# Routing the rows of a mixture of experts in five parts instead of two

## The chip, the cores and the metric

The kernel runs on one core of a Trainium2 chip. The metric is the device time of one execution in microseconds (us), the median of several runs. TensorE does the matrix products and transposes, VectorE (DVE in the profile) the elementwise work, ScalarE (ACT) activations and copies out of PSUM, GpSimd (POOL) issues the DMAs whose addresses come from a table in SBUF, SyncE (SP) issues the plain DMAs.

## The reference

The input is `x` of shape (2, 64, 64, 256), so two batches of 4096 tokens. A first layer (deformable attention with sampled keys and values) and an attention with one-dimensional convolutions come first; they take some nine tenths of the time and are not touched here. The last piece is a mixture of eight experts:

```python
logits = x @ gate_w + gate_b                      # x: 8192 tokens, 256 channels, after a layer norm
probs = softmax(logits)
idx = argmax(probs); prb = probs[idx]
one_hot = one_hot(idx, 8)
pos = (cumsum(one_hot, axis=0) * one_hot).sum(-1) - 1   # place of the token in its expert's list
kept = pos < C                                    # C = 1280 places for each expert
buf = zeros(8, C, 256).at[idx, pos].set(x)        # dropped where not kept
y = relu(buf @ w1 + b1) @ w2 + b2                 # expert by expert
out = t + y[idx, pos] * (prb * kept)
```

The place of a token depends on all tokens before it, through the running sum over the tokens. That sum can be made in parts, if each part begins with the counts that the parts before it have reached.

## The kernel before

`stage_mix_route` is the stage before the experts, `stage_experts` the last one. Each stage ends with a barrier over all engines (`Stage.__exit__`), and the expert stage begins with loads from `s["buf"]`, the table into which the tokens' rows are scattered. So all scatters have to be complete before the expert stage can start.

The mixing stage goes over 16 chunks of 512 tokens (`STEPS` = 16), eight for each batch; a chunk is four tiles of 128 tokens (`GT` = 4). Each loop step `n` runs on all engines:

- TensorE: `convolve(n)` (24 matmul records, the output projection), then `gates(n - 1)` (transposes of the normalized tiles and the gate logits of the chunk before), then `turn_out(n)` (transposes back to tokens by channels).
- VectorE: `share_out(n + 2)` (a product for a later chunk), `got_gates(n - 1)`, `residual(n)`, `normalize(n)`, which writes the rows `h` of the chunk.
- ScalarE: copies of `oT` and `hT` out of PSUM and the square root in `std`.
- SyncE stores the chunk and loads a later one.

Routing comes on top. `choose` (VectorE) finds each token's expert from the gates and leaves it as zeros and ones in `hot`. `count` (TensorE) multiplies `hot` by a triangular matrix and by a matrix of ones, which gives the running counts inside a tile and the totals of each tile in `ps_n`. `exponentials` (ScalarE) makes the exponentials of the softmax. `send` (VectorE) makes the token's probability, sums the tiles' totals in a scan that doubles its step, adds what is in `seen` from before, and writes the row number of each token to `to_row`. GpSimd waits for that (`rows_made`) and issues one indirect DMA for each tile of 128 tokens, which writes 128 rows of 264 numbers to `s["buf"]`.

Before the change this is done once for each batch: part 0 has the 32 tiles of batch 0, and its `choose` stands at step 8 and its `send`, `count` and `exponentials` at step 9. Part 1 has the 32 tiles of batch 1, and all of it stands behind the loop, since the last chunk's gates are needed. The order on each engine is the order in which the code is written; each engine waits only for semaphores.

Of the kernel before, what the change touches and what calls it, by code (L numbers as in the profile page):

```python
# [29 lines left out]
CHUNKS = N // CHUNK  # L30
# [10 lines left out]
E, F, CAP = 8, 4 * C, 5 * B * N // (4 * 8)  # L41
# [579 lines left out]
class Sampling:  # L621
# [235 lines left out]
    PARTS = 6  # L857
# [1253 lines left out]
def stage_mix_route(nc, d, s, keep, out):  # L2111


    with Stage(nc) as stack:
        r = Room(nc, stack, "x")
        ALL, GT, XS = B * TILES, CHUNK // P, 3
        STEPS, QS = B * CHUNKS, B * QBS
        inverse = Inverse(r, s, 1)
        ctx = [r.sb(f"ctx{b}", [P, CH, N + 2]) for b in range(B)]
        share = [r.sb(f"share{i}", [P, CH, QB]) for i in range(2)]  # L2120
# [3 lines left out]
        h = r.sb("h", [P, ALL, ROW])  # L2124
# [95 lines left out]

        @block.tensor
        def _(pe):
# [38 lines left out]
                            mm = pe.matmul(ps_g[:, i * E:(i + 1) * E], hT[i % 2][:, m, :], gw[:, m, :], start=(m == 0), stop=(m == CH - 1))  # L2261
                        mm.then_inc(g_mm, 1)

            def count(b):
                if b == 0:
                    pe.wait_ge(route_in, 80)
                else:
                    pe.wait_ge(count_got, b)
                pe.wait_ge(hot_made, b + 1)
                flat = hot[:, :, :].rearrange("p t e -> p (t e)")  # L2270
                pe.matmul(ps_n[:, 0, :], upper[:, :], flat, start=True, stop=True)
                pe.matmul(ps_n[:, 1, :], ones[:, :], flat, start=True, stop=True).then_inc(counted, 1)

            pe.wait_ge(edges, 2 * B)
            pe.wait_ge(consts, 80)
            for n in range(STEPS + 1):
                if n < STEPS:
                    convolve(n)
                if n:
                    gates(n - 1)  # L2280
                if n < STEPS:
                    turn_out(n)
                if n == CHUNKS + 1:
                    count(0)
            count(1)

        @block.scalar
        def _(act):
            def exponentials(b):
                act.wait_ge(less, b + 1)  # L2290
                act.activation(exps[:, :, :], exps[:, :, :], ACT.Exp).then_inc(exped, 1)
# [24 lines left out]
        def _(dve):  # L2316
# [43 lines left out]
            def tokens(v):  # L2360
                return v[:, :].unsqueeze(2).to_broadcast([P, TILES, E])

            def experts(v):
                return v[:, :].unsqueeze(1).to_broadcast([P, TILES, E])

            def tt(o, a, z, op):
                t.link(dve.tensor_tensor(o, a, z, op))

            def choose(b):
                gate = keep.gate[:, b * TILES:(b + 1) * TILES, :]  # L2370
                dve.wait_ge(g_got, CHUNKS * (b + 1))
                dve.wait_ge(route_in, 80)
                if b:
                    dve.wait_ge(rows_made, b)
                t.link(dve.tensor_reduce(top[:, :], gate, AX_X, ALU.max))

                tt(hot[:, :, :], gate, tokens(top), ALU.is_equal)
                tt(hot[:, :, :], hot[:, :, :], experts(prio), ALU.mult)
                t.link(dve.tensor_reduce(best[:, :], hot[:, :, :], AX_X, ALU.max))
                tt(rank[:, :, :], hot[:, :, :], tokens(best), ALU.is_equal)  # L2380
                dve.tensor_copy(hot[:, :, :], rank[:, :, :]).then_inc(hot_made, 1)
                dve.tensor_tensor(exps[:, :, :], gate, tokens(top), ALU.subtract).then_inc(less, 1)

            def send(b):
                own = slice(b * TILES, (b + 1) * TILES)
                dve.wait_ge(exped, b + 1)
                t.link(dve.tensor_reduce(total[:, :], exps[:, :, :], AX_X, ALU.add))
                t.link(dve.reciprocal(prob[:, :], total[:, :]))
                t.link(dve.tensor_copy(h[:, own, C], prob[:, :]))
                t.link(dve.tensor_copy(h[:, own, C + 1], number[:, own]))  # L2390
                dve.wait_ge(counted, b + 1)
                flat = "p t e -> p (t e)"
                t.link(dve.tensor_copy(each[:, :, :].rearrange(flat), ps_n[:, 1, :]))
                t.link(dve.tensor_copy(before[:, :, :], each[:, :, :]))

                step, src, dst = 1, before, work
                while step < TILES:
                    t.inc(dve.tensor_copy(dst[:, 0:step, :], src[:, 0:step, :]))
                    tt(dst[:, step:, :], src[:, step:, :], src[:, 0:TILES - step, :], ALU.add)
                    step, src, dst = 2 * step, dst, src  # L2400
                if b:
# [3 lines left out]
                tt(src[:, :, :], src[:, :, :], each[:, :, :], ALU.subtract)  # L2405
                dve.tensor_tensor(src[:, :, :].rearrange(flat), src[:, :, :].rearrange(flat), ps_n[:, 0, :], ALU.add).then_inc(count_got, 1)
                dve.wait_ge(count_got, b + 1)
                dve.wait_ge(hot_made, b + 1)
                tt(src[:, :, :], src[:, :, :], hot[:, :, :], ALU.mult)
                t.link(dve.tensor_reduce(place[:, :], src[:, :, :], AX_X, ALU.add))  # L2410
                tt(hot[:, :, :], hot[:, :, :], experts(first), ALU.mult)
                t.link(dve.tensor_reduce(expert[:, :], hot[:, :, :], AX_X, ALU.add))
                t.link(dve.tensor_scalar(kept[:, :], place[:, :], float(CAP), None, ALU.is_lt))

                t.link(dve.tensor_scalar(total[:, :], kept[:, :], -float(2 * E * CAP), float(2 * E * CAP), ALU.mult, ALU.add))
                t.link(dve.tensor_scalar(place[:, :], place[:, :], float(CAP - 1), None, ALU.min))
                tt(row[:, :], expert[:, :], place[:, :], ALU.add)
                dve.tensor_tensor(to_row[:, own], row[:, :], total[:, :], ALU.add).then_inc(rows_made, 1)

            t.link(dve.memset(h[:, :, C:], 0.0))  # L2420
            share_out(0)
# [15 lines left out]
            choose(1)  # L2437
            send(1)


def stage_attention(nc, d, s, keep, b, c, row_max, sa, begin, flow):
# [370 lines left out]
```

## Time and profile before

| | us |
|---|---|
| median of 3 runs | 9658.51 (9646.36, 9658.51, 9661.88) |
| the profiled execution, its own time | 9657.97 |
| its span (first to last instruction) | 9656.2 |
| TensorE busy | 7727.8 (80%) |
| VectorE busy | 5175.6 (54%) |
| GpSimd busy | 5070.2 (53%) |
| ScalarE busy | 3767.1 (39%) |

The span is what the timelines count from; 1.8 us of the execution's time lie outside it. The mixing stage's first TensorE instruction starts at 8684.43 us, the expert stage's first at 9027.93 us. The busy shares are means over stages with different limits, so the stretch around the change has to be read by itself.

### The profile page before, as it was taken

How to read it: one execution, taken by the hardware profiler on the slowest of the kernel's cores; microseconds unless marked ns; L12 is line 12 of the kernel's file. 1: busy time of each engine (PE TensorE's matmuls, PEld its weight loads, DVE VectorE, ACT ScalarE, POOL GpSimd, SP SyncE). 2: the span in 40 equal slices, each digit the busy share in tenths (PEclk: the TensorE clock that was granted, in tenths of full speed). 3: DMA queues.
4: the chain of work that ended last, by engine and by line, in shares of the span. 5: the costliest groups of instructions: out<-in, count | busy, mean ns of one | idle time of the engine just before them, and what ended most of it. 6: DMA issues, size and time to landing. Idle time of an engine off the chain costs nothing. (4 is left out here: it accounts for less than half of the span.)

```text
span 9656.2 us, 96652 instructions
## 1 busy us (share of the span) xinstructions
PE 7727.8 (80%) x31522; PEld 4168.2 (43%) x31522; DVE 5175.6 (54%) x10029; ACT 3767.1 (39%) x5495; POOL 5070.2 (53%) x4864
## 2 busy tenths in 40 slices
PE   7637776645894799869999977997999799989699
PEld 3623333433442344434444433443444344435466
DVE  6543335545564566656666555665653466634233
ACT  2101102201462266525666533662666255541232
POOL 1057777667777777777777777777730000001322
PEclk9868888867897799988999988997999799999799
DMA  3844335666543544454444355445430311115221
GB/s 129 289 150 137 120 119 178 213 217 211 161 138 112 175 138 144 130 179 126 138 139 146 119 176 180 142 129 178 137 101 28 94 46 46 40 45 157 81 73 54
DMA packets 658546, 1283.59 MB, mean 133 GB/s; under 512 B 189043, under 2 KB 398218, under 8 KB 643408
## 3 DMA queue, kind: packets, MB, share of 16 engines
q0 software_dynamic: 234240, 639.57, 21.2%
q1 hardware_dynamic: 405392, 562.58, 19.5%
q10 hardware_dynamic: 18432, 75.51, 2.0%
q8 instruction: 243, 3.98, 0.2%
q14 instruction: 239, 1.96, 0.1%
HBM read 1003.44 MB, written 278.91 MB: 133 GB/s over the span
## 5 line engine op out<-in xcount | busy, mean ns | idle before, releaser
L727 POOL DMA_INDIRECT sa_slot<-s_table,sa_rec x4608 | 4812.6, 1044 | 2279.2 <-issue 1382.9
L1704 DVE CUSTOM_DVE_ANT_0 a_above<-a_late,a_above 128x512 f32<-128x512 f32 x1600 | 1101.6, 689 | 1436.5 <-PE a_late L1556 1321.5
L1636 ACT ACTIVATE a_p<-a_s 128x1024 f32<-128x1024 f32 x1600 | 1628.6, 1020 | 124.4 <-PE a_s L1594 122.6
L1611 PE MATMUL a_ctx<-a_p,a_v 128*64 128x512 f32 x6400 | 1577.3, 614 | 85.0 <-issue 84.5
L1645 ACT ACTIVATE a_above<-a_diff 128x512 f32<-128x512 f32 x1600 | 956.6, 598 | 1648.2 <-PE a_diff L1544 1379.7
L769 DVE TENSOR_TENSOR sa_slot<-sa_slot,sa_q 128x1152 f32<-128x1152 f32 x512 | 694.0, 1355 | 1021.6 <-DMA sa_slot<-s_table,sa_rec 1005.1
L1594 PE MATMUL a_s<-a_q,a_k 98*128 98x512 f32 x3200 | 1047.3, 411 | 3.2 <-ACT a_p L1636 3.2
L878 PE MATMUL sa_sums<-keep_ident,sa_vals 128*128 128x128 f32 x4608 | 681.3, 297 | 420.9 <-DVE sa_vals L821 420.9
L1556 PE MATMUL a_late<-a_k,a_q 96*128 96x512 f32 x1600 | 815.2, 510 | 168.0 <-DVE a_pair_max L1704 164.6
L1544 PE MATMUL a_diff<-a_kd,a_q 96*128 96x512 f32 x1600 | 725.5, 453 | 194.8 <-DMA a_q<-s_q 157.6
L878 PEld LDWEIGHTS sa_sums<-keep_ident,sa_vals 128*128 128x128 f32 x4608 | 609.5, 155 | 518.6 <-DVE sa_vals L821 439.4
L2211 POOL MEMSET x_ctx<- 128x2 f32 x2 | 0.2, 106 | 1529.6 <-POOLq L77 1529.6
L1556 PEld LDWEIGHTS a_late<-a_k,a_q 96*128 96x128 f32 x1600 | 318.7, 199 | 1046.1 <-issue 632.5
L1611 PEld LDWEIGHTS a_ctx<-a_p,a_v 128*64 128x64 f32 x6400 | 403.6, 138 | 830.9 <-issue 695.8
L2032 DVE TENSOR_REDUCE a_chunk_max<-a_max 128x1 f32<-128x512 f32 x896 | 552.7, 680 | 309.2 <-PE a_max L1908 309.2
L775 DVE TENSOR_REDUCE sa_dots<-sa_slot 128x36 f32<-128x1152 f32 x512 | 690.7, 1349 | 11.5 <-ACT p_vT L1253 4.6
L821 DVE TENSOR_TENSOR sa_vals<-sa_slot,sa_corner 128x1152 f32<-128x1152 f32 x512 | 681.3, 1354 | 1.8
L1594 PEld LDWEIGHTS a_s<-a_q,a_k 98*128 98x128 f32 x3200 | 583.9, 192 | 130.6 <-ACT a_p L1636 31.4
L1983 ACT ACTIVATE a_p<-a_s 128x1024 f32<-128x1024 f32 x448 | 454.8, 1024 | 452.7 <-PE a_s L1941 447.3
L1210 PE MATMUL p_c<-p_hT,p_w 128*128 128x512 f32 x1152 | 520.6, 610 | 8.0 <-DMA p_wb<-in_bqkv 7.0
L1544 PEld LDWEIGHTS a_diff<-a_kd,a_q 96*128 96x128 f32 x1600 | 322.2, 201 | 309.5 <-DMA a_q<-s_q 159.9
L1908 PE MATMUL a_max<-a_k,a_q 96*128 96x512 f32 x896 | 378.7, 476 | 64.5 <-DVE a_chunk_max L2032 40.5
(280 smaller groups left out, 8089.3 us busy)
## 6 DMA issues: line engine op xcount, KB each, us to landing
sa_slot<-s_table,sa_rec POOLq DMA_INDIRECT x4608, 3.1
s_table<-t_rows ACTq DMA_DIRECT2D x64, 1024.0 KB, 7.7
a_q<-s_q SPq DMA_DIRECT2D x480, 128.0 KB, 3.5
s_part<-a_o SPq DMA_DIRECT2D x160, 256.0 KB, 2.4
t_qwin<-s_dwq SPq DMA_DIRECT2D x64, 512.0 KB, 6.9
t_kvwin<-s_dwkv SPq DMA_DIRECT2D x64, 386.0 KB, 10.3
a_kd<-s_kd SPq DMA_DIRECT2D x384, 64.0 KB, 3.4
a_o<-s_part SPq DMA_DIRECT2D x96, 256.0 KB, 3.6
```

What stands on the lines that cost most here:

```text
L727: pool.indirect_dma_start(out=self.slot[g][:, k, :, :, :].rearrange("p c a n -> p (c a n)"), out_offset=None, in_=self.s["table"][n // TIL ...
L769: t.inc(dve.tensor_tensor(k, k, q, ALU.mult))
L775: t.inc(dve.tensor_reduce(self.dots[g // 4][:, g % 4, :, :].rearrange("p k c -> p (k c)"), k, AX_X, ALU.add))
L821: dve.tensor_tensor(self.vals[:, :, j * HC:(j + 1) * HC], v, w.to_broadcast([P, 4 * K, HC]), ALU.mult)\
L878: mm = pe.matmul(self.ps_sum[i], self.vals[:, j, :], self.keep.ident[:, :], start=(j == 0), stop=(j == 4 * K - 1), is_transpose=True)
L1544: pe.matmul(self.ps_diff, self.q[run.n % self.QR][0:3 * HD, t * P:(t + 1) * P], self.kd_tile(run.head, g)[:, :], start=True, stop=True).th ...
L1556: pe.matmul(self.ps_late, self.q[run.n % self.QR][0:3 * HD, t * P:(t + 1) * P], self.k[run.head % self.KR][0:3 * HD, at:at + CHUNK], start ...
L1594: mm = pe.matmul(self.ps_s[slot % 2][:, i * CHUNK:(i + 1) * CHUNK], self.k[run.head % self.KR][:, kb * P:(kb + 1) * P], self.q[run.n % sel ...
L1611: mm = pe.matmul(self.ps_ctx[i * 2 * HD:(i + 1) * 2 * HD, :], self.v_and_ones(run.head, kb), self.p[slot % P_SLOTS][:, i * CHUNK:(i + 1) * ...
L1636: act.activation(self.p[slot % P_SLOTS][:, :], self.ps_s[slot % 2], ACT.Exp, scale=float(HD) ** -0.5).then_inc(self.exped, 1)
L1645: act.activation(self.above[slot % n][:, :], self.ps_diff, ACT.Relu).then_inc(self.diff_got, 1)
L1704: dve.tensor_tensor_reduce(above, self.ps_late, above, 1.0, LOWEST, ALU.add, ALU.max, self.pair_max[:, t, j:j + 1]).then_inc(self.late_got, 1)
```

## The change

A list `ENDS = [4, 8, 12, 14, 16]` gives the chunk at which each of five parts ends; the parts have 16, 16, 16, 8 and 8 tiles. `choose(part)` now stands at steps 4, 8, 12 and 14, `send`, `count` and `exponentials` at steps 5, 9, 13 and 15, and those of the last part behind the loop. Every operation of a part works on as many tiles as the part has, the scan takes four doublings for 16 tiles and three for 8 (five for 32 before), and `seen` is added and renewed in every part. GpSimd waits once for each part.

```diff
+        ENDS = [4, 8, 12, 14, STEPS]
+        PARTS = len(ENDS)
+        def tiles_of(part):
+            return slice(GT * ENDS[part - 1] if part else 0, GT * ENDS[part])
...
@@ gpsimd
-            for b in range(B):
-                pool.wait_ge(rows_made, b + 1)
-                for t in range(b * TILES, (b + 1) * TILES):
+            for part in range(PARTS):
+                pool.wait_ge(rows_made, part + 1)
+                for t in range(tiles_of(part).start, tiles_of(part).stop):
                     pool.indirect_dma_start(
...
@@ tensor
-            def count(b):
+            def count(part):
...
-                pe.wait_ge(hot_made, b + 1)
-                flat = hot[:, :, :].rearrange("p t e -> p (t e)")
-                pe.matmul(ps_n[:, 0, :], upper[:, :], flat, start=True, stop=True)
-                pe.matmul(ps_n[:, 1, :], ones[:, :], flat, start=True, stop=True).then_inc(counted, 1)
+                pe.wait_ge(hot_made, part + 1)
+                flat = hot[:, 0:size_of(part), :].rearrange("p t e -> p (t e)")
+                pe.matmul(ps_n[:, 0, 0:size_of(part) * E], upper[:, :], flat, start=True, stop=True)
+                pe.matmul(ps_n[:, 1, 0:size_of(part) * E], ones[:, :], flat, start=True, stop=True).then_inc(counted, 1)
...
-                if n == CHUNKS + 1:
-                    count(0)
-            count(1)
+                if n - 1 in ENDS:
+                    count(ENDS.index(n - 1))
+            count(PARTS - 1)
...
@@ scalar
-                if n == CHUNKS + 1:
-                    exponentials(0)
-            exponentials(1)
+                if n - 1 in ENDS:
+                    exponentials(ENDS.index(n - 1))
+            exponentials(PARTS - 1)
...
@@ vector
-            def choose(b):
-                gate = keep.gate[:, b * TILES:(b + 1) * TILES, :]
-                dve.wait_ge(g_got, CHUNKS * (b + 1))
+            def choose(part):
+                m = size_of(part)
+                gate = keep.gate[:, tiles_of(part), :]
+                dve.wait_ge(g_got, ENDS[part])
...
-                while step < TILES:
+                while step < m:
...
-                if b:
-                    tt(src[:, :, :], src[:, :, :], experts(seen), ALU.add)
-                else:
-                    t.link(dve.tensor_copy(seen[:, :], src[:, TILES - 1, :]))
+                if part:
+                    tt(src[:, 0:m, :], src[:, 0:m, :], experts(seen, m), ALU.add)
+                t.link(dve.tensor_copy(seen[:, :], src[:, m - 1, :]))
...
-                if n == CHUNKS:
-                    choose(0)
-                if n == CHUNKS + 1:
-                    send(0)
-            choose(1)
-            send(1)
+                if n - 1 in ENDS:
+                    send(ENDS.index(n - 1))
+                if n in ENDS and n < STEPS:
+                    choose(ENDS.index(n))
+            choose(PARTS - 1)
+            send(PARTS - 1)
```

GpSimd's queue in the mixing stage, before the change, one row for each piece that runs without a wait (the semaphore's number had another name in an earlier stage; it is `rows_made` here):

```order
L2216 DMA s_buf<-x_h,x_to_row 10240x264 [waits p01_lm]
L2216 DMA s_buf<-x_h,x_to_row 10240x264 x31
L2216 DMA s_buf<-x_h,x_to_row 10240x264 [waits p01_lm]
L2216 DMA s_buf<-x_h,x_to_row 10240x264 x31
```

And the same queue after the change:

```order
L2225 DMA s_buf<-x_h,x_to_row 10240x264 [waits p01_lm]
L2225 DMA s_buf<-x_h,x_to_row 10240x264 x15
L2225 DMA s_buf<-x_h,x_to_row 10240x264 [waits p01_lm]
L2225 DMA s_buf<-x_h,x_to_row 10240x264 x15
L2225 DMA s_buf<-x_h,x_to_row 10240x264 [waits p01_lm]
L2225 DMA s_buf<-x_h,x_to_row 10240x264 x15
L2225 DMA s_buf<-x_h,x_to_row 10240x264 [waits p01_lm]
L2225 DMA s_buf<-x_h,x_to_row 10240x264 x7
L2225 DMA s_buf<-x_h,x_to_row 10240x264 [waits p01_lm]
L2225 DMA s_buf<-x_h,x_to_row 10240x264 x7
```

The 64 DMAs are the same; behind the last wait stand 8 of them where 32 stood.

TensorE at the end of the stage, before the change, from the last `turn_out` (`x_ps_t`) over the last chunk's gates to the count (`x_ps_n`):

```order
L2243 MATMUL x_ps_t<-keep_ident,x_oT 128x128 x8
L2256 MATMUL x_ps_h<-keep_ident,x_h 128x128 x4
L2261 MATMUL x_ps_g<-x_gw,x_hT 128x8 x4
L2256 MATMUL x_ps_h<-keep_ident,x_h 128x128 x4
L2261 MATMUL x_ps_g<-x_gw,x_hT 128x8 x4
L2271 MATMUL x_ps_n<-x_hot,x_upper 128x256
L2272 MATMUL x_ps_n<-x_hot,x_ones 128x256
```

And the same place after the change:

```order
L2252 MATMUL x_ps_t<-keep_ident,x_oT 128x128 x8
L2280 MATMUL x_ps_n<-x_hot,x_upper 128x64
L2281 MATMUL x_ps_n<-x_hot,x_ones 128x64
L2265 MATMUL x_ps_h<-keep_ident,x_h 128x128 x4
L2270 MATMUL x_ps_g<-x_gw,x_hT 128x8 x4
L2265 MATMUL x_ps_h<-keep_ident,x_h 128x128 x4
L2270 MATMUL x_ps_g<-x_gw,x_hT 128x8 x4
L2280 MATMUL x_ps_n<-x_hot,x_upper 128x64
L2281 MATMUL x_ps_n<-x_hot,x_ones 128x64
```

A count of eight tiles (64 columns) has come in ahead of the last gates, and the count behind them is of 64 columns instead of 256. On VectorE the 25 instructions of the fourth part's `send` stand in the same way between the last chunk's `normalize` and its `got_gates`.

## Rows read from the trace of the kernel before

**Rows 1.** Stretches: length, busy PE, PEld, DVE, ACT, POOL; clock, DMA share, GB/s.
```profile
8940.00:8950.00 10.00, 5.72 (x27) 4.93 (x28) 5.44 (x18) 1.01 (x4) 0.00 (x0) 0.51 0.31 105
...
8990.00:9000.00 10.00, 0.00 (x0) 0.00 (x0) 0.00 (x0) 0.00 (x0) 7.56 (x9) 0.50 0.29 104
...
9020.00:9030.00 10.00, 1.95 (x8) 1.36 (x8) 0.86 (x5) 0.86 (x3) 0.18 (x1) 0.50 1.05 364
...
9040.00:9050.00 10.00, 10.00 (x30) 5.51 (x30) 0.00 (x0) 4.48 (x8) 7.56 (x9) 1.00 0.20 56
```

**Rows 2.** Timeline of GpSimd: start us, us, engine, line, operation, [idle before <- releaser].
```profile
8857.73 1.16 POOL L2216 DMA_INDIRECT s_buf<-x_h,x_to_row  x1 [202.21 <-DVE x_to_row L2418]
...
8866.86 1.49 POOL L2216 DMA_INDIRECT s_buf<-x_h,x_to_row  x1 [0.30 <-issue]
...
8898.62 0.97 POOL L2216 DMA_INDIRECT s_buf<-x_h,x_to_row  x1 [0.30 <-issue]
8966.73 0.97 POOL L2216 DMA_INDIRECT s_buf<-x_h,x_to_row  x1 [67.13 <-DVE x_to_row L2418]
...
9006.34 0.97 POOL L2216 DMA_INDIRECT s_buf<-x_h,x_to_row  x1 [0.30 <-issue]
```

**Rows 3.** Timeline of SyncE at the start of the expert stage.
```profile
9015.24 0.35 SPq L2540 DMA_DIRECT2D e_spare<-in_spare  x1
```

**Rows 4.** Timeline of VectorE after the last chunk.
```profile
8953.29 0.19 DVE L2330 TENSOR_TENSOR keep_gate<-x_ps_g,x_gb 128x32 f32<-128x32 f32 x1 [5.04 <-PE x_ps_g L2261]
...
8955.80 0.29 DVE L2381 COPY x_hot<-x_rank 128x256 f32<-128x256 f32 x1
...
8965.76 0.19 DVE L2418 TENSOR_TENSOR x_to_row<-x_row,x_total 128x32 uint32<-128x32 f32 x1
```

**Rows 5.** Timeline of VectorE in loop step 9.
```profile
8848.26 0.42 DVE L2387 TENSOR_REDUCE x_total<-x_exps 128x32 f32<-128x256 f32 x1
...
8852.54 0.28 DVE L2367 TENSOR_TENSOR x_work<-x_before 128x128 f32<-128x128 f32 x1
8852.86 0.17 DVE L2404 COPY x_seen<-x_work 128x8 f32<-128x8 f32 x1
8853.07 0.43 DVE L2367 TENSOR_TENSOR x_work<-x_work,x_each 128x256 f32<-128x256 f32 x1
...
8856.68 0.19 DVE L2418 TENSOR_TENSOR x_to_row<-x_row,x_total 128x32 uint32<-128x32 f32 x1
...
8859.32 0.19 DVE L2330 TENSOR_TENSOR keep_gate<-x_ps_g,x_gb 128x32 f32<-128x32 f32 x1 [1.31 <-PE x_ps_g L2261]
```

**Rows 6.** Timeline of TensorE in the mixing loop.
```profile
8713.24 10.47 PE L2231 MATMUL x_ps_o<-x_ctx,x_w 128*128 128x512 f32 x24
...
8728.30 10.47 PE L2231 MATMUL x_ps_o<-x_ctx,x_w 128*128 128x512 f32 x24
...
8842.81 1.06 PE L2271 MATMUL x_ps_n<-x_hot,x_upper 128*128 128x256 f32 x2
...
8844.51 10.55 PE L2231 MATMUL x_ps_o<-x_ctx,x_w 128*128 128x512 f32 x24
...
8860.88 12.60 PE L2231 MATMUL x_ps_o<-x_ctx,x_w 128*128 128x512 f32 x24
```

**Rows 7.** Timeline of ScalarE in loop steps 9 and 10.
```profile
8858.07 1.28 ACT L2310 ACT_TABLE_LOAD   x1
8864.35 0.20 ACT L2310 ACTIVATE x_std<-x_var 128x4 f32<-128x4 f32 x1 [5.00 <-DVE x_var L2353]
```

**Rows 8.** Chain of waits in the expert stage: start us, us, what.
```profile
9020.62 7.26 DMA e_b<-in_b
...
9034.24 37.12 PE e_ps_m L2590 x96
...
9112.03 34.66 PE e_ps_m L2590 x96
...
9263.08 37.04 PE e_ps_m L2590 x96
```

More of the change, by code:

```diff
@@ L2117, in stage_mix_route, with size_of @@
         STEPS, QS = B * CHUNKS, B * QBS
+        ENDS = [4, 8, 12, 14, STEPS]
+        PARTS = len(ENDS)
+        def tiles_of(part):
+            return slice(GT * ENDS[part - 1] if part else 0, GT * ENDS[part])
+        def size_of(part):
+            own = tiles_of(part)
+            return own.stop - own.start
         inverse = Inverse(r, s, 1)
@@ L2282, in _, with exponentials @@
                     turn_out(n)
-                if n == CHUNKS + 1:
-                    count(0)
-            count(1)
+                if n - 1 in ENDS:
+                    count(ENDS.index(n - 1))
+            count(PARTS - 1)
         @block.scalar
         def _(act):
-            def exponentials(b):
-                act.wait_ge(less, b + 1)
-                act.activation(exps[:, :, :], exps[:, :, :], ACT.Exp).then_inc(exped, 1)
+            def exponentials(part):
+                own = exps[:, 0:size_of(part), :]
+                act.wait_ge(less, part + 1)
+                act.activation(own, own, ACT.Exp).then_inc(exped, 1)
             for n in range(STEPS + 1):
@@ L2358, in normalize, with tokens, experts @@
                                       ALU.subtract, ALU.mult).then_inc(h_made, 1)
[L2360 to L2364, printed above, removed]
+            def tokens(v, m):
+                return v[:, 0:m].unsqueeze(2).to_broadcast([P, m, E])
+            def experts(v, m):
+                return v[:, :].unsqueeze(1).to_broadcast([P, m, E])
             def tt(o, a, z, op):
@@ L2384, in send @@
[L2384 to L2389, printed above, removed]
+                if part:
+                    dve.wait_ge(rows_made, part)
+                t.link(dve.tensor_reduce(top[:, 0:m], gate, AX_X, ALU.max))
+                tt(hot[:, 0:m, :], gate, tokens(top, m), ALU.is_equal)
@@ new lines, in choose, with send @@
+                tt(hot[:, 0:m, :], hot[:, 0:m, :], experts(prio, m), ALU.mult)
+                t.link(dve.tensor_reduce(best[:, 0:m], hot[:, 0:m, :], AX_X, ALU.max))
+                tt(rank[:, 0:m, :], hot[:, 0:m, :], tokens(best, m), ALU.is_equal)
+                dve.tensor_copy(hot[:, 0:m, :], rank[:, 0:m, :]).then_inc(hot_made, 1)
+                dve.tensor_tensor(exps[:, 0:m, :], gate, tokens(top, m), ALU.subtract).then_inc(less, 1)
+            def send(part):
+                m, own = size_of(part), tiles_of(part)
+                dve.wait_ge(exped, part + 1)
+                t.link(dve.tensor_reduce(total[:, 0:m], exps[:, 0:m, :], AX_X, ALU.add))
+                t.link(dve.reciprocal(prob[:, 0:m], total[:, 0:m]))
+                t.link(dve.tensor_copy(h[:, own, C], prob[:, 0:m]))
@@ L2390, in send @@
                 t.link(dve.tensor_copy(h[:, own, C + 1], number[:, own]))
-                dve.wait_ge(counted, b + 1)
+                dve.wait_ge(counted, part + 1)
                 flat = "p t e -> p (t e)"
-                t.link(dve.tensor_copy(each[:, :, :].rearrange(flat), ps_n[:, 1, :]))
-                t.link(dve.tensor_copy(before[:, :, :], each[:, :, :]))
+                t.link(dve.tensor_copy(each[:, 0:m, :].rearrange(flat), ps_n[:, 1, 0:m * E]))
+                t.link(dve.tensor_copy(before[:, 0:m, :], each[:, 0:m, :]))
@@ L2396, in send @@
                 step, src, dst = 1, before, work
-                while step < TILES:
+                while step < m:
                     t.inc(dve.tensor_copy(dst[:, 0:step, :], src[:, 0:step, :]))
-                    tt(dst[:, step:, :], src[:, step:, :], src[:, 0:TILES - step, :], ALU.add)
+                    tt(dst[:, step:m, :], src[:, step:m, :], src[:, 0:m - step, :], ALU.add)
                     step, src, dst = 2 * step, dst, src
-                if b:
-                    tt(src[:, :, :], src[:, :, :], experts(seen), ALU.add)
-                else:
-                    t.link(dve.tensor_copy(seen[:, :], src[:, TILES - 1, :]))
@@ L2405, in send @@
[L2405 to L2418, printed above, removed]
+                if part:
+                    tt(src[:, 0:m, :], src[:, 0:m, :], experts(seen, m), ALU.add)
@@ new lines, in send @@
+                t.link(dve.tensor_copy(seen[:, :], src[:, m - 1, :]))
+                tt(src[:, 0:m, :], src[:, 0:m, :], each[:, 0:m, :], ALU.subtract)
+                dve.tensor_tensor(src[:, 0:m, :].rearrange(flat), src[:, 0:m, :].rearrange(flat), ps_n[:, 0, 0:m * E], ALU.add)\
+                    .then_inc(count_got, 1)
+                dve.wait_ge(count_got, part + 1)
+                dve.wait_ge(hot_made, part + 1)
+                tt(src[:, 0:m, :], src[:, 0:m, :], hot[:, 0:m, :], ALU.mult)
@@ new lines, in send @@
+                t.link(dve.tensor_reduce(place[:, 0:m], src[:, 0:m, :], AX_X, ALU.add))
+                tt(hot[:, 0:m, :], hot[:, 0:m, :], experts(first, m), ALU.mult)
+                t.link(dve.tensor_reduce(expert[:, 0:m], hot[:, 0:m, :], AX_X, ALU.add))
+                t.link(dve.tensor_scalar(kept[:, 0:m], place[:, 0:m], float(CAP), None, ALU.is_lt))
+                t.link(dve.tensor_scalar(total[:, 0:m], kept[:, 0:m], -float(2 * E * CAP), float(2 * E * CAP), ALU.mult, ALU.add))
+                t.link(dve.tensor_scalar(place[:, 0:m], place[:, 0:m], float(CAP - 1), None, ALU.min))
@@ L2420, in _ @@
+                tt(row[:, 0:m], expert[:, 0:m], place[:, 0:m], ALU.add)
+                dve.tensor_tensor(to_row[:, own], row[:, 0:m], total[:, 0:m], ALU.add).then_inc(rows_made, 1)
             t.link(dve.memset(h[:, :, C:], 0.0))
```

12 lines of the change are left out of this document (2 added, 10 removed).

## The prediction

> **What bounds the kernel now.** The busy shares over the whole span say little here, so I read the end of the mixing stage by itself. The first view is busy time in stretches of 10 us [rows 1]. The reader is to see that between 8990 and 9000 us only GpSimd works: TensorE, VectorE and ScalarE have 0.00 busy, GpSimd 7.56 us, the DMA engines a share of 0.29. In the stretches at 9020 and 9040 TensorE comes back. The second view is GpSimd's timeline [rows 2]. GpSimd waits 67.13 us for `to_row`, and then issues 32 indirect DMAs, from 8966.73 to 9006.34 + 0.97 = 9007.31 us. The pitch is (9006.34 − 8966.73) / 31 = 1.278 us, of which 0.97 us is the instruction and 0.30 us the gap behind it. SyncE's first DMA of the expert stage follows at 9015.24 [rows 3], 7.93 us after the end of the last issue: landing, barrier and clearing of semaphores. TensorE starts only when the first expert's loads land, at 9020.62 + 7.26 [rows 8]. So the end of the mixing stage is a serial chain: last gates (8953.29, [rows 4]), `choose` and `send` (to_row done at 8965.76 + 0.19 = 8965.95), 32 issues, 7.93 us, loads. The first 32 issues lie beside the loop (8857.73 to 8899.59, [rows 2]) and delay nothing there.
>
> The loop itself is bound by TensorE: one step takes 8728.30 − 8713.24 = 15.06 us at full clock, and 8860.88 − 8844.51 = 16.37 us where the granted clock dips [rows 6].
>
> **Term 1, the issues behind the last wait.** 24 of the 32 go. Their place is not simply 24 x 1.278 = 30.7 us, because the eight issues of the part before are now close ahead, and `send` gets shorter; so I follow the times, in the old trace's clock.
>
> *When part 3 (chunks 12, 13) is ready.* Its `send` stands right behind the last `normalize`, and VectorE had nothing else to do there: it idled 5.04 us before `got_gates` at 8953.29 [rows 4], so from 8948.25. I let `send` start at 8948.3. For 32 tiles `send` took 8856.68 + 0.19 − 8848.26 = 8.61 us in 28 instructions [rows 5]. For 8 tiles it has 25 (four scan instructions fewer, one addition of `seen` more). The prices: 0.43 us for 256 elements, 0.28 for 128, 0.17 for 8, so about 0.23 for 64 and 0.17 to 0.19 for the narrow ones, plus 0.04 between dependent ones. Fourteen wide ones at 0.27 and eleven narrow ones at 0.2, less 0.6 for the copies that overlap in the scan, gives 5.4 us (in the same way 6.6 us for 16 tiles). Bounds: 25 x 0.17 = 4.3, and 8.6 as for 32 tiles. Ready at 8953.7.
>
> *GpSimd.* The first issue follows `to_row` by 0.8 us (8966.73 − 8965.95, and 8857.73 − 8856.87 = 0.86). So part 3's eight issues run from 8954.5 to 8954.5 + 8 x 1.278 = 8964.7. Earlier parts are out of the way: part 2's `send` begins two steps of 16.4 us earlier, near 8915.5, ends near 8922, and 16 issues take 20.4 us, to 8943.
>
> *When part 4 is ready.* `got_gates(15)` was at 8953.29 waiting for TensorE; VectorE is now in `send` until 8953.7, so it slips 0.4 us. Then 0.2 us for `got_gates`, 1.5 us for `choose` (2.6 before, from 8953.48 to 8955.80 + 0.29, [rows 4]), 0.6 us until the exponentials are there, and 5.4 us for `send`: `to_row` is done near 8961.5, 4.4 us earlier than the old 8965.95. That is before GpSimd is free (8964.7). What ends last there is therefore GpSimd's own queue: 16 issues in a row from 8954.5, the last one ending at 8954.5 + 15 x 1.278 + 0.97 = 8974.6. Against 9007.31 that is **−32.7 us**. If `send` costs its upper bound, part 3 starts 3.2 us later: −29.5. At the lower bound −33.8.
>
> **Term 2, the counts in the loop.** TensorE runs without gaps there, so they lie on its path. One count of 256 columns took 8844.51 − 8842.81 = 1.70 us [rows 6]. Before there is one in the loop. Now there are three of 128 columns (0.85 each by columns) and one of 64 at step 15, in a hole: TensorE was busy for 5.72 us of the 10 from 8940, waiting for `h` in the rest, [rows 1]. Sum 3 x 0.85 − 1.70 = **+0.9 us**. Bounds: 0 if matmuls hide in the neighbours, 3 x 1.70 − 1.70 = +3.4 if the width doesn't matter.
>
> **Term 3, VectorE in the loop.** `send` stands behind `normalize(n)`, so it can't delay `h(n)`. It delays `share_out` and `got_gates(n)`. At step 9 the 32-tile version, 8.61 us, still left 1.31 us of waiting for TensorE before `got_gates` (8859.32, [rows 5]). The 16-tile versions are shorter (6.6 us), so cover remains: 0. Without that cover each would cost TensorE its overhang once, bound +2 us over three.
>
> **Term 4, ScalarE.** Each `exponentials` brings a change of function table and one back. The change back took 1.28 us at 8858.07, and then ScalarE idled 5.00 us before the next `std` (8864.35, [rows 7]): hidden, 0. At step 15 the table load and the exponentials stand ahead of the last `hT` copies and reach about their start: 0 to +0.3 us. In return, the last exponentials need no load.
>
> **Term 5, the expert stage.** It starts as before, with the same rows and loads. 7.93 us and 7.26 us stay: the DMA engines' share in the tail was 0.29 [rows 1], so I expect no backlog that shrinks or grows. TensorE's clock is at 0.50 in the idle stretch and until the first expert's matmuls (37.12 us against 34.66 for the next expert, [rows 8]); TensorE's idle time before it becomes 32 us shorter, but some 38 us of it remain, and the clock fell to 0.51 in the stretch at 8940 already, so I expect it cold again. 0, bound −2.5 us if it came warm.
>
> **Sum.** −32.7 + 0.9 = −31.8 us. From the profiled execution: 9657.97 − 31.8 = 9626.2; the median lies 0.5 us above it, so 9627 us. Bounds of the terms: −33.8 − 2.5 = −36.3, and −29.5 + 3.4 + 2 + 0.3 = −23.8. The three runs lie 15.5 us apart, which adds some 8 us either way: 9614 to 9643.
>
> **A rule against it.** In the loop, GpSimd's issues run beside VectorE work, in the tail they did not. The row: of the 32 issues beside the loop two took 1.5 us (1.49 at 8866.86) and all of them 41.86 us, against 40.58 in the tail [rows 2]: 1.3 us for 32, so half a microsecond for the last 16. The Trainium skill ("SBUF — State Buffer", "Who interferes with whom") says that VectorE in a two-port mode, which its copies and tensor-scalar operations can enter, and GpSimd hold a shared pair of ports exclusively, the later one blocked for the whole instruction of the other. By that rule some ten such instructions of the last `choose` and `send` would each wait up to 0.97 us for a running issue, half of that on average.
>
> **Rivals.**
>
> *R1, the two engines hold each other up.* Part 3's issues run beside the last `choose` and `send`. If ten VectorE instructions lose 0.5 to 1 us each, `to_row` comes at 8966.5 to 8971.5 instead of 8961.5, later than GpSimd is free, and the end moves by 2.6 to 7.6 us: 9630 to 9635, centre 9632. For it: the 1.49 us issues. Against it: 32 issues beside a VectorE that is busy about half the time lost 1.3 us altogether.
>
> *R2, routing on VectorE holds the loop.* If three sends of 16 tiles ran late enough to leave TensorE idle 2 us each, and the clock fell and came back as after the idle stretch, each would cost 2 us and some 5 us of slower matmuls (10 us at half speed), 21 in all: 9648. Against it: 1.31 us were left even beside the 32-tile `send`. It needs a `send` over 9.9 us.
>
> *R3, the clock takes part of it back.* A step of the loop with a dip of the clock costs 16.37 − 15.06 = 1.3 us more than one without [rows 6]. The expert stage comes after a long rest and was granted 1.00 at 9040 [rows 1]; the matmuls of one expert took 34.66 us, those of two others 37.1 [rows 8]. With 32 us less rest more dips may enter it: ten at 1.3 us give 9640.
>
> *R4, slower.* The same place, but the whole expert stage runs as the loop did: (9656.2 − 9034.2) / 16.4 = 38 dips, at 1.3 us (loop) to 2.4 us (37.04 − 34.66, [rows 8]) each, 49 to 91 us, middle 70: 9627 + 70 = 9697. It decides from 32 us, so from 13 to 24 dips. Against it: the first two experts have one slow set of matmuls between them, the first, right behind the rest; the next slow one begins at 9263.08 [rows 8].
>
> *R5, part 4 does not become short*, because GpSimd still has a backlog from the middle parts. That would need part 2's issues to last past 8953, 10 us longer than worked out; each microsecond beyond costs one. Within the forecast's range.
>
> **Chances.** Forecast 0.80, R1 0.07, R2 0.04, R3 0.06, R4 0.03. About 0.2% (19 us, so 9639 us) is what a measurement can tell from no change. Forecast and R1 are faster than that but for a tail of 0.02 from scatter between runs: faster 0.85. R2, R3 and that tail: same 0.12. R4: slower 0.03. The range reaches from the lower bound with scatter, 9614, to R3 and the upper bound, 9643; it leaves out R2, R4 and the ends.
>
> **What the profile after would show.** Right: GpSimd issues in five groups of 16, 16, 16, 8, 8; the last 16 in one run with gaps of 0.30 us and no wait for `to_row` ahead of the last eight; SyncE's first DMA of the expert stage 31 to 33 us earlier and 7.9 us after the last issue; loop steps of 15.1 to 16.4 us with no idle time of TensorE at steps 6, 10 and 14; matmuls of the count 0.4 to 0.5 us for 128 columns. Wrong: a wait of GpSimd ahead of the last eight (R1 or a longer `send`), TensorE waiting for `h` or `shared` behind steps 5, 9, 13 (R2), granted clock under 1.00 in more than two stretches of the expert stage (R3, R4), or 7.93 us that become longer.

## The result, and the profile after

| | before | after |
|---|---|---|
| median of 11 runs | 9669.93 us (9646.36 to 9681.66) | 9628.25 us (9612.56 to 9649.58) |
| profiled execution, span | 9656.2 us | 9620.1 us |

The ratio is 0.9961, with a 95% interval from 0.9952 to 0.9971: 28 to 46 us faster, 38 us in the middle. The forecast of 9627 us was for a base of 9658.5 us, the median of the three runs known then; with more runs the base rose by 11 us, so the forecast's −32 us is to be held against −38 us (−42 us between the two medians of the table, −36.1 us between the two spans), and not 9627 against 9628. That these two agree to 1 us is luck: the base was 11 us too low, and the gain was larger than forecast.

GpSimd's timeline after the change answers to [rows 2]. The columns are start, duration, engine, line, operation, and in brackets the idle time before it with what ended it:

```profile
8793.74 1.16 POOL L2225 DMA_INDIRECT s_buf<-x_h,x_to_row  x1 [137.02 <-DVE x_to_row L2429]
...
8860.32 1.20 POOL L2225 DMA_INDIRECT s_buf<-x_h,x_to_row  x1 [45.66 <-DVE x_to_row L2429]
...
8927.04 0.97 POOL L2225 DMA_INDIRECT s_buf<-x_h,x_to_row  x1 [45.85 <-DVE x_to_row L2429]
...
8956.25 0.97 POOL L2225 DMA_INDIRECT s_buf<-x_h,x_to_row  x1 [9.06 <-DVE x_to_row L2429]
...
8965.19 0.97 POOL L2225 DMA_INDIRECT s_buf<-x_h,x_to_row  x1 [0.30 <-issue]
8966.47 0.97 POOL L2225 DMA_INDIRECT s_buf<-x_h,x_to_row  x1 [0.30 <-issue]
...
8975.41 0.97 POOL L2225 DMA_INDIRECT s_buf<-x_h,x_to_row  x1 [0.30 <-issue]
```

There are five parts, but only four unbroken runs: the row at 8966.47 is the first issue of the last part, and it has the same 0.30 us ahead of it as any other. GpSimd was still busy with the part before when the last rows became ready. The last issue ends at 8975.41 + 0.97 = 8976.38 us, where it was 9007.31. What follows keeps its length, as SyncE's timeline (against [rows 3]) shows, 7.92 us where it was 7.93:

```profile
8984.30 0.35 SPq L2551 DMA_DIRECT2D e_spare<-in_spare  x1
```

The forecast called these 7.9 us landing, barrier and clearing of semaphores. The trace's records of the sequencers, which the timelines leave out, say where they go: the last DMA has landed 1.4 us after the end of its issue, and then GpSimd executes a DRAIN instruction of 5.28 us, the same before and after the change.

VectorE at the end of the stage, against [rows 4]. The first two rows are the fourth part's `send` from its first instruction to its last, the third is `got_gates` of the last chunk, the last is the end of the whole routing:

```profile
8950.13 0.22 DVE L2398 TENSOR_REDUCE x_total<-x_exps 128x8 f32<-128x64 f32 x1
...
8955.30 0.17 DVE L2429 TENSOR_TENSOR x_to_row<-x_row,x_total 128x8 uint32<-128x8 f32 x1
8955.39 0.18 DVE L2340 TENSOR_TENSOR keep_gate<-x_ps_g,x_gb 128x32 f32<-128x32 f32 x1
...
8958.08 0.42 DVE L2400 COPY x_h<-x_prob 128x8 f32<-128x8 f32 x1
...
8963.07 0.17 DVE L2429 TENSOR_TENSOR x_to_row<-x_row,x_total 128x8 uint32<-128x8 f32 x1
```

`send` for eight tiles took 8955.30 + 0.17 − 8950.13 = 5.34 us. `got_gates` follows with no idle time in the row: VectorE is what it waited for, as forecast, if only by 0.2 us (it starts 5.23 us behind the last `h`, before the change 5.04). The last `to_row` is there at 8963.24, 3.2 us before GpSimd takes it up.

TensorE's counts in the loop, against [rows 6]:

```profile
8781.10 0.64 PE L2280 MATMUL x_ps_n<-x_hot,x_upper 128*128 128x128 f32 x2
8781.53 0.64 PE L2281 MATMUL x_ps_n<-x_hot,x_ones 128*128 128x128 f32 x2
8781.96 11.69 PE L2240 MATMUL x_ps_o<-x_ctx,x_w 128*128 128x512 f32 x24
...
8914.10 0.39 PE L2280 MATMUL x_ps_n<-x_hot,x_upper 128*128 128x128 f32 x2
8914.32 0.39 PE L2281 MATMUL x_ps_n<-x_hot,x_ones 128*128 128x128 f32 x2
8914.55 10.47 PE L2240 MATMUL x_ps_o<-x_ctx,x_w 128*128 128x512 f32 x24
...
8949.29 1.09 PE L2265 MATMUL x_ps_h<-keep_ident,x_h 128*128 128x128 f32 x4 [4.08 <-issue]
```

The two matmuls of 128 columns together take 0.86 us at step 5, from the first's start to the start of what follows (records of 0.64 us each), and 0.45 us at step 13 (0.39 us each). The granted clock was 0.50 at step 5 and 1.00 at step 13.

ScalarE at step 13, against [rows 7]: table load and exponentials, then the load back, which is over long before the next square root (idle 3.97 us):

```profile
8918.00 1.28 ACT L2301 ACT_TABLE_LOAD   x1
8919.29 0.31 ACT L2301 ACTIVATE x_exps<-x_exps 128x128 f32<-128x128 f32 x1
8919.96 0.60 ACT L2309 ACTIVATE x_oT<-x_ps_o 128x512 f32<-128x512 f32 x1 [0.36 <-PE x_ps_o L2240]
...
8928.02 1.28 ACT L2320 ACT_TABLE_LOAD   x1
8933.27 0.21 ACT L2320 ACTIVATE x_std<-x_var 128x4 f32<-128x4 f32 x1 [3.97 <-DVE x_var L2363]
```

The chain of waits in the expert stage, against [rows 8]:

```profile
8989.64 7.32 DMA e_b<-in_b
...
9003.30 34.66 PE e_ps_m L2601 x96
...
9078.63 34.66 PE e_ps_m L2601 x96
...
9380.34 37.03 PE e_ps_m L2601 x96
```

The chain before the change has a third slow set, which [rows 8] leave out:

```profile
9491.85 37.00 PE e_ps_m L2590 x96
```

The first expert's first matmuls take 34.66 us instead of 37.12, and behind them only one of the seven others is slow, where it was two.

Where the 36.1 us between the two spans are:

| piece | before | after | difference |
|---|---|---|---|
| start of the mixing loop's first matmul | 8684.43 | 8685.02 | +0.59 |
| from there to the end of the last `h` | 263.82 | 265.14 | +1.32 |
| from there to the end of the last issue | 59.06 | 26.22 | −32.84 |
| from there to TensorE's restart | 20.62 | 20.62 | 0.00 |
| expert stage | 628.27 | 623.10 | −5.17 |

### The profile page after: what moved, and what is told of

Its sections match the earlier page's. It is cut to its first block and busy times, and to the rows that moved or that the text cites. A ratio compares the mean times of both kernels' runs of the same rounds, so it can differ in the third digit from the quotient of the medians.

```text
span 9620.1 us, 96790 instructions
## 1 busy us (share of the span) xinstructions
PE 7716.2 (80%) x31534; PEld 4162.1 (43%) x31534; DVE 5191.0 (54%) x10124; ACT 3772.2 (39%) x5502; POOL 5078.2 (53%) x4864
## 6 DMA issues: line engine op xcount, KB each, us to landing
t_kvwin<-s_dwkv SPq DMA_DIRECT2D x64, 386.0 KB, 10.3
```

## The experiments

Two theories stand against each other over the tail, and two over the clock.

- *Queue theory* (that of the prediction): what counts is the number of issues that GpSimd has in its last unbroken run, 1.278 us each, beginning with the `to_row` that starts it. Rivals: the number of tiles in the last part; the spreading of the scatters over the loop; the shorter last `send`.
- *Clock theory* (formed after the result): the 2.46 us at the first expert come from TensorE's shorter rest, 38 us instead of 70. Rival: it is chance.

The first eight kernels ran on two chips (the four up to "Four tiles in the last part" on one, the other four on the second) on which all kernels, that of before among them, took about 11800 us instead of 9660 us. The 2100 us are lost ahead of the mixing stage, nearly all in the first layer's indirect loads: the 4500th indirect DMA is issued at 6972 us in the changed kernel's first profile and at 8992 us in its profile there. Why is not known. The tails that can be compared (five parts, six parts, 24 issues more) have the same length on both kinds of chip to 0.12 us, so tails are compared, but the ratios have intervals of 0.25 to 0.4% either way and tell little. The last three kernels ran on a chip like the first.

**Two parts again.** The one edit that undoes the change:

```diff
-        ENDS = [4, 8, 12, 14, STEPS]
+        ENDS = [8, STEPS]
```

> Five parts taken back to two (ends 8 and 16), all else as in the changed code. Queue theory (what counts is the number of issues in GpSimd's last unbroken run): 32 issues behind the last wait again, last issue near 9007 us, SyncE's first load of the expert stage near 9015, time like the kernel before (ratio 1.000 +- 0.001). Clock theory (part of the gain comes from a TensorE that is warm sooner after a shorter rest): the first expert's first matmuls take 37.1 us again, after 70 us of rest. Rival (the phase of the clock against the kernel is chance): 34.66 or 37.1, without regard to the rest.

From the end of the last `h` to the end of the last issue 59.33 us (59.06 before). GpSimd's last run, first and last of 32:

```profile
11130.74 0.97 POOL L2225 DMA_INDIRECT s_buf<-x_h,x_to_row  x1 [88.57 <-DVE x_to_row L2429]
...
11170.42 0.97 POOL L2225 DMA_INDIRECT s_buf<-x_h,x_to_row  x1 [0.30 <-issue]
```

The ratio to before was 0.9983, [0.9952, 1.0014]. The new code by itself brings the tail nothing (it costs 0.3 us, one copy of `seen` more); the ends of the parts do. The first expert's first matmuls, which the expectation names, took 38.7 us here, neither 37.1 nor 34.66; on these two chips they took 38.6 to 42.1 us in all eight profiles, more than the level of the clock accounts for, so they decide nothing about the clock, and the moment of its return is used below instead.

**Only the first batch split.**

```diff
+        ENDS = [4, 8, STEPS]
```

> Ends 4, 8, 16: only the first batch is split, the last part keeps 32 tiles. Queue theory: no gain in the tail, time as before (ratio 1.000 +- 0.001), since the earlier issues were hidden. Rival (spreading the scatters over the loop is itself worth something): 5 to 10 us faster than before. First expert's first matmuls 37.1 us by the clock theory, since the rest stays 70 us.

The tail is 59.33 us again, with 32 issues in the last run. The ratio was 0.9968, [0.9943, 0.9994], which taken alone would speak for the rival; but the interval nearly touches 1, the scatter of this chip is 100 us and more, and no row of the tail moved. From its first matmul to the last `h` the loop took 276.5 us in this profile, and 287.2 to 289.0 us in the other three of this chip; one profile doesn't tell whether that is the split or chance. I take from it that splitting early does nothing for the tail, and leave open whether it does anything else.

**Only the second batch split, at 14.**

```diff
+        ENDS = [8, 14, STEPS]
```

> Ends 8, 14, 16: the first batch whole, the second in 24 and 8 tiles. The 24-tile part is sent at step 15, close ahead of the last part. Queue theory: its to_row comes near 8957 us (7.5 us for send), and GpSimd then has 24 + 8 = 32 issues in a row, 41 us, last one ending near 8998: 9 us faster than before, 22 us slower than the five parts. Rival (what counts is the number of tiles in the last part): 8 tiles in the last part, so the full gain of 31 us.

This is the experiment that parts the queue from the size of the last part. GpSimd's last run, of which the 25th issue (at 11205.55) is the first of the last part:

```profile
11174.87 0.97 POOL L2225 DMA_INDIRECT s_buf<-x_h,x_to_row  x1 [79.91 <-DVE x_to_row L2429]
...
11205.55 0.97 POOL L2225 DMA_INDIRECT s_buf<-x_h,x_to_row  x1 [0.30 <-issue]
...
11214.49 0.97 POOL L2225 DMA_INDIRECT s_buf<-x_h,x_to_row  x1 [0.30 <-issue]
```

The last part has 8 tiles as in the changed kernel, and still the tail is 49.46 us and not 26.2: 32 issues run without a break, because the 24 ahead of them could not start earlier. That is 23.2 us more than with five parts, where 22 were expected by the queue and none by the rival. The number of tiles in the last part is not what counts. Ratio 0.9981, [0.9951, 1.0011].

**Four tiles in the last part.**

```diff
+        ENDS = [4, 8, 12, 15, STEPS]
```

> Ends 4, 8, 12, 15, 16: 12 tiles in the part before the last, 4 in the last. Queue theory: the 12-tile part can be sent only behind got_gates of the last chunk, to_row near 8961.5, then 16 issues in a row from 8962.3 to 8982.5, 6 us later than with five parts at 14, so 25 us faster than before. Rival (size of the last part): 4 issues fewer than with 8 tiles, 5 us faster than five parts at 14.

```profile
11131.31 0.97 POOL L2225 DMA_INDIRECT s_buf<-x_h,x_to_row  x1 [25.68 <-DVE x_to_row L2429]
...
11146.66 0.97 POOL L2225 DMA_INDIRECT s_buf<-x_h,x_to_row  x1 [0.30 <-issue]
...
11150.50 0.97 POOL L2225 DMA_INDIRECT s_buf<-x_h,x_to_row  x1 [0.30 <-issue]
```

One run of 16 (the 13th, at 11146.66, is the first of the last part) with a tail of 32.20 us, 5.98 us longer than with five parts, where 6 were expected. A smaller last part made it slower, since the part before it becomes ready only behind the last gates. Ratio 0.9972, [0.9936, 1.0008].

**24 issues more.** The opposite test: five parts, and only the removed issues put back.

```diff
+            for again in s["again"]:      # three more tables in memory, read by nobody
+                for t in range(tiles_of(PARTS - 1).start, tiles_of(PARTS - 1).stop):
+                    pool.indirect_dma_start(out=again, ...).then_inc(sent, 16)
... (and the wait for `sent` counts the 24 too)
```

> Five parts, and behind the last part's 8 issues 24 more of the same rows, into three other tables in memory that nobody reads. This puts back the 24 issues that the change took from behind the last wait, and nothing else of it. Queue theory: last issue 24 x 1.278 = 30.7 us later, the whole gain of the tail gone: time as the kernel before plus 0 to 1 us. Rival (the shorter send and choose, or the spreading, carry a good part of the gain): still 5 us or more faster than before. Rest of TensorE 69 us, so by the clock theory the first expert's first matmuls take 37.1 us.

> The 24 issues put back behind the last part once more. Queue theory: ratio 1.000 +- 0.001, stage's end 66.8 us behind the last h as before the change (67.0). Rival (spreading or shorter routing steps carry part of the gain): 0.9990 or less.

GpSimd's last run, on the second occasion: first issue, last of the 16, first and last of the added ones; and SyncE behind it.

```profile
8955.05 0.97 POOL L2225 DMA_INDIRECT s_buf<-x_h,x_to_row  x1 [9.06 <-DVE x_to_row L2434]
...
8974.23 0.97 POOL L2225 DMA_INDIRECT s_buf<-x_h,x_to_row  x1 [0.30 <-issue]
8975.51 0.97 POOL L2230 DMA_INDIRECT s_again<-x_h,x_to_row  x1 [0.30 <-issue]
...
9004.92 0.97 POOL L2230 DMA_INDIRECT s_again<-x_h,x_to_row  x1 [0.30 <-issue]
```

```profile
9015.77 0.35 SPq L2556 DMA_DIRECT2D e_spare<-in_spare  x1
```

The added run goes on at the same pitch, (9004.92 − 8975.51) / 23 = 1.279 us. SyncE starts 66.81 us after the last `h`, before the change 66.99 us. This agreement is made of two parts. From the last `h` to the end of the last issue are 56.93 us, 2.1 us less than the 59.06 of before: 30.7 us of the tail's 32.84 are the 24 issues, and the rest goes with the last run's earlier start. (Here that run starts 12.4 us earlier than before the change and has eight issues more, which take 10.2.) From there to SyncE are 9.88 us, 2.0 us more than the 7.91 or 7.92 of the eleven other profiles, since GpSimd's DRAIN took 7.24 us instead of 5.28, with 88 indirect DMAs in the stage instead of 64. Whether it grew by their number or by the three new tables is not known.

The ratio was 1.0002, [0.9964, 1.0040] on a slower chip and 0.9995, [0.9985, 1.0004] on the one like the first: with the 24 issues back, the gain is gone. The total can't see the 2.1 us, which the longer DRAIN covers, and a part of up to 14 us for the spreading is still inside the interval. The forecast's Term 1 is shown by the tail's rows, and the total agrees.

**The changed kernel again**, as a yardstick for the others.

> The changed kernel once more, beside the next three on one chip. Queue theory: from the end of the last h to the end of the last issue 26.2 us, where the kernel before has 59.1. The total 31 us faster, and up to 5 us more or less by where the dips of TensorE's clock fall. Clock theory: the first expert's first matmuls take 34.66 us because the rest is 38 us instead of 70; by chance theory they take 34.66 or 37.1 from profile to profile.

> The changed kernel as the yardstick of this chip. Tail 26.2 us from the end of the last h. Queue theory: ratio 0.9966 (33 us of the tail less 0.5 us of counts), in an interval that holds 1 only if the chip scatters as the last one did. The clock's return behind the rest: by chance theory anywhere from 5 to 12 us after the restart.

Tails of 26.26 and 26.22 us. The clock came back 4.7 and 9.0 us after the restart. Ratios 0.9976, [0.9943, 1.0009] and, on the chip like the first, 0.9955, [0.9942, 0.9967]. The second middle value is −43 us, which is more than the 33 us of the tail; its interval begins at −32.

**Matmuls in the rest.** 18 matmuls on TensorE behind the last count, so that it rests 20.48 us and not 38.5.

```diff
+            for i in range(18):
+                mm = pe.matmul(ps_o[0][:, :], w[:, 0, 0, 0:P], w[:, 0:2, :, 0:P], start=True, stop=True)
... (and TensorE waits for the last one to end)
```

> Five parts, and behind the last count 18 matmuls of 512 columns on TensorE whose results nobody reads, some 0.9 us each at the lower clock, 16 us in all, from 8958.5 to 8974.5, beside GpSimd's last issues. No lengthening of the stage by the queue theory (the last issue ends at 8976.4). Clock theory: rest of 22 us instead of 38, so the clock comes back at 1.00 no later after the restart than the 5.4 us seen with five parts, perhaps at once (2 us less). Chance theory: anything from 5 to 11 us.

The stage did not get longer (tail 26.26 us). The matmuls took 18.35 us in all:

```profile
11030.57 18.35 PE L2298 MATMUL x_ps_o<-x_w 128*128 128x512 f32 x36
```

They did more than shorten the rest. The granted clock rose to 1.00 5.4 us after their start, stayed there for 4.1 us after their end at 11048.93, and then fell to 0.50. In the other profiles the clock was at 0.50 already when the rest began. Even so the clock theory, in which the length of the rest decides, fell. These rows are stretches of this kernel (columns as in [rows 1]), the last being that in which the clock came back, at 11080.34; the restart was at 11069.41, 10.9 us before, a long time after the shortest rest of all:

```profile
11069.00:11071.00 2.00, 1.48 (x6) 1.00 (x6) 0.86 (x5) 0.75 (x2) 0.00 (x0) 0.50 1.08 388
11079.00:11080.00 1.00, 1.00 (x2) 0.34 (x1) 0.00 (x0) 0.47 (x1) 0.79 (x1) 0.50 0.79 265
11080.00:11081.00 1.00, 1.00 (x3) 0.48 (x2) 0.12 (x1) 0.22 (x1) 0.70 (x2) 0.83 0.21 70
```

For comparison the changed kernel, which restarted at 8997.00 and was back within 6 us after a rest of 38.5 us:

```profile
9001.00:9002.00 1.00, 0.95 (x6) 0.55 (x4) 0.00 (x0) 0.68 (x2) 0.69 (x2) 0.50 1.02 414
9002.00:9003.00 1.00, 0.83 (x4) 0.29 (x3) 0.00 (x0) 0.60 (x3) 0.70 (x2) 0.57 0.99 373
9003.00:9004.00 1.00, 0.70 (x2) 0.46 (x3) 0.00 (x0) 0.25 (x1) 0.88 (x1) 1.00 1.07 396
```

Rest and time until the clock's return, in us, over all thirteen profiles:

| rest | clock back after |
|---|---|
| 20.5 (with matmuls ahead of it) | 10.9 |
| 36.0, 36.2 | 9.9, 8.6 |
| 38.5 (after), 38.5, 38.9, 39.0 | 5.9, 9.0, 8.6, 4.7 |
| 60.2 | 5.9 |
| 69.6 (before), 70.4, 71.0, 71.2, 71.2 | 11.3, 9.1, 9.1, 11.3, 10.7 |

After rests of one length, 38.5 to 39.0 us, the clock took anything from 4.7 to 9.0 us. The rests of 36 to 39 us have a mean of 7.8 us, those of 70 us one of 10.3, which would be 1.2 us of TensorE time; the 60.2 us and the 20.5 us speak against an order. So of the 2.46 us some may belong to the change and the rest is scatter; the runs don't part them.

**Six parts.** The queue theory points to a better split: four tiles less at step 15 leave GpSimd idle when the last `to_row` comes.

```diff
+        ENDS = [4, 8, 12, 13, 14, STEPS]
```

> Ends 4, 8, 12, 13, 14, 16: the 8-tile part before the last is cut in two of 4 tiles, one sent at step 14, one at step 15. Queue theory: at step 15 only 4 issues start (5.1 us), so GpSimd is idle when the last part's to_row comes, and the last issue ends 0.8 + 7 x 1.278 + 0.97 = 10.7 us behind that to_row: 23.7 us from the end of the last h instead of 26.2, so 2.5 us faster than five parts. Rival (the count and the send of one part more cost as much as they save, 0.5 us on TensorE and up to 2 us of VectorE in step 14): 0 to 1 us.

> Ends 4, 8, 12, 13, 14, 16 once more, since the total could not tell 2.5 us. From the end of the last h to the end of the last issue 23.4 us, as measured; ratio to the kernel before 0.9960 if the total has the tail's 35.6 us and the clock's dips fall evenly. Rival (the sixth part costs the loop what it saves): ratio as with five parts.

```profile
8946.49 0.97 POOL L2225 DMA_INDIRECT s_buf<-x_h,x_to_row  x1 [7.51 <-DVE x_to_row L2429]
...
8950.33 0.97 POOL L2225 DMA_INDIRECT s_buf<-x_h,x_to_row  x1 [0.30 <-issue]
8954.79 0.97 POOL L2225 DMA_INDIRECT s_buf<-x_h,x_to_row  x1 [3.49 <-DVE x_to_row L2429]
...
8963.74 0.97 POOL L2225 DMA_INDIRECT s_buf<-x_h,x_to_row  x1 [0.30 <-issue]
```

Four issues, then a wait of 3.49 us for the last `to_row`, then eight. The tail is 23.44 and 23.54 us, 2.7 to 2.8 us shorter, where 2.5 were expected. The total is not: ratios 0.9994, [0.9955, 1.0033] and 0.9972, [0.9962, 0.9982], and medians 6 and 16 us above those of five parts on the same chips. In the second profile the loop from its first matmul to the last `h` took 269.41 us at a mean granted clock of 0.91. Three profiles of kernels whose loop has five parts gave 261.9 (0.93), 264.6 (0.91) and 265.1 us (0.92), and the kernel before 263.8 (0.91). The extra count in the loop explains 0.7 us of the 4 to 7 us. Most of the rest goes with more work at the lower clock, which two digits of a mean hide: TensorE was busy at 0.50 for 50.0 us of this loop, and for 35.6, 42.7 and 42.2 us of the three. On a slower chip the six-part loop was the longer one too, 292.5 us against 283.6 to 286.6. Whether the sixth part brings that or it fell so by chance, two profiles don't settle. Six parts don't beat five by what was measured.

## Why the prediction was right

*Term 1, the issues behind the last wait: right, in mechanism and size.* From the end of the last `h` the forecast had 8974.6 − 8948.25 = 26.35 us; measured were 26.22, 26.26, 26.22. Its steps held too: `send` for eight tiles 5.34 us (5.4), 0.78 us to the first issue (0.8), `to_row` of the last part 13.08 us behind the last `h` (13.25), GpSimd taking it up 3.2 us later. The experiments with the ends at 14 alone and at 15 show that this was not luck: the same way of adding up gave 22 and 6 us more than five parts, and 23.2 and 6.0 were measured. SyncE's first DMA came 30.94 us earlier, just short of the 31 to 33 named as a sign, because the last `h` was there 1.9 us later.

*Term 2, the counts: right in sign, and in size by chance of the clock.* In the first profile +0.46 us (0.86 + 0.85 + 0.45 − 1.70) and not +0.9. The 1.70 us of before was measured in a dip of the clock, and the forecast took it as the price of columns without saying at which level. It holds at the lower level (0.85 us for 128 columns); at full clock the same width costs 0.45 us. In the third profile of five parts all three counts fell into dips, and the term was the +0.85 us of the forecast. Of the loop's +1.32 us about half a microsecond goes with more work at the lower clock (TensorE busy at 0.50 for 42.2 us instead of 41.1); the remaining 0.3 us no row assigns. The forecast's steps of at most 16.4 us were not seen: they took up to 17.3 us, and up to 18.1 before the change.

*Term 3, VectorE in the loop: right.* Behind the 16-tile `send`s of steps 5, 9 and 13 VectorE waited another 3.49, 2.58 and 2.61 us for TensorE, and behind that of 8 tiles none, as forecast. TensorE's idle time in the loop did not grow (16.5 us, 16.6 before).

*Term 4, ScalarE: right.* 3.97 us were left behind the load back. At step 13 the next copy waited 0.36 us for TensorE, so at this width even ScalarE's table load had just enough room. At step 15 TensorE's last gates ended 5.0 us behind the last `h`, as before the change.

*Term 5, the expert stage: zero was forecast, −5.17 us measured.* One part is the bound that was named: −2.46 us, the clock back sooner. The other is one slow set of matmuls fewer, 2.4 us. By the means over the thirteen profiles about half of the first, 1.2 us, may belong to the change, and none of it is shown to; a later profile of the changed kernel had 35.96 us there, with the clock back after 9.0 us.

*R1, the two engines hold each other up: seen, and too small to count.* The copy at 8958.08 took 0.42 us instead of the 0.17 us of its neighbour, one of four such rows; together 0.5 us, with 3.2 us of cover. By the Trainium skill's rule ("SBUF — State Buffer", "Who interferes with whom") each could have been held for a whole issue of 0.97 us. The trace agrees in kind and not in amount. Three of the four rows end together with the issue beside them (at 8957.24, 8958.50 and 8959.77, the issues at 8957.22, 8958.49 and 8959.77) and had begun 0.64, 0.55 and 0.75 us into it; copies that began 0.20 to 0.42 us into an issue kept their length. So in this profile a copy was held for the last part of an issue, never for a whole one. GpSimd is held too: its four issues longer than 1.1 us (1.16, 1.48, 1.20 and 1.48) all began while VectorE's 1.22 us product in `share_out` was under way, and each ended 0.84 to 0.88 us behind that product. No such product stands behind the last chunk, and no issue of the last 16 took more than 0.97 us.

*R2, R3, R4* did not come: no wait of TensorE for `h` or `shared`, and behind the first set one slow set of matmuls in the expert stage where two had been.

What stays open is the difference between the ratios' middle values (−38 and −43 us) and the 32 us that the stage gives. Both intervals reach down to about that (−28 and −32), and 5 us of the expert stage's dips came in the first profile; more than that no row shows.

## What to carry to other kernels

Where a stage ends in a queue of small DMAs from one engine, count the issues in the last unbroken run of that queue and price them by the pitch of the trace; the last part's size alone misleads, since the part ahead of it may still stand in the queue. Split so that the part before the last is issued when the last one becomes ready. And take no price of a matmul from a row without looking at the granted clock of that moment.

## What the runs showed of the hardware

- GpSimd issues one indirect DMA of 128 rows every 1.278 us, on all chips, and the small operations of `choose` and `send` beside it don't change that (16 issues from 8956.25 to 8975.41, 1.277 us each, the first six beside VectorE). An issue that began during VectorE's 1.22 us product was longer, up to 1.49 us instead of 0.97 (1.80 us in the third profile of five parts).
- GpSimd's DRAIN at the end of this stage took 5.28 us with 64 indirect DMAs in the stage, whatever the length of the last run (8 to 32), and 7.24 us in the two profiles with 88; it makes up most of the 7.92 us from the last issue to the next stage's first DMA.
- After a rest, TensorE's granted clock came back from 0.50 (1.2 GHz) to 1.00 (2.4 GHz) between 4.7 and 11.3 us after the restart, with no strict order in rests of 20 to 71 us. On the chips with the shorter times it made up to 2.5 us in the first expert's matmuls. In the one kernel that worked in the rest, the clock rose to 1.00 after 5.4 us of matmuls and fell 4.1 us after the last.
- On two chips every kernel took 22% longer, with TensorE's mean granted clock at 0.82 instead of 0.90, while the tail of the mixing stage kept its length to 0.12 us. A difference of 30 us could be read from the profile there, and not from the times.
